# Shifted-window attention stage: scores in 32x64 tiles in two groups, transposes in two row tiles, group norm folded into projections, half of the maxima subtracted by GpSimd

## The chip, the cores and the metric

The kernel runs on one core of a Trainium2 chip. The metric is the time of one launch in microseconds (us). Engines are written as in the profile: PE (TensorE), PEld (its weight loads), DVE (VectorE), ACT (ScalarE), POOL (GpSimd), SP (the queue that issues the DMAs).

## The reference

The input is 16 images of 56x56 positions with 192 channels. Two blocks follow each other. The first, which the change does not touch, is a group norm, a layer norm, a scan over the 49 positions of each 7x7 window and an MLP. The second, cut to what matters:

```python
x = x + L1(gn(x))                       # gn: 32 groups of 6 channels, per image
# L1: windows of 7x7 shifted by 3, 12 heads of 16 dimensions
qkv  = xw @ qkv_w.T + qkv_b             # 1024 windows x 49 tokens x 576
attn = einsum('bhnd,bhmd->bhnm', q * 16**-0.5, k) + bias + mask
attn = softmax(attn, axis=-1)
out  = einsum('bhnm,bhmd->bhnd', attn, v) @ proj_w.T + proj_b
```

## The kernel before

The first block runs for some 2430 us. The second has 128 units of eight windows each (`UNITS`); a unit u has four steps p = 0 to 3 (`UP`), each with two windows of 49 tokens that lie in 64-row slots. Below, k = 4u + p numbers the steps. Every engine runs its own `slot(i, c, r)` once per unit, its instructions in the order in which they are written, and they meet by semaphores that count up; there is no scheduler. The engines work on different steps at a time. In step k:

- PE computes the scores of step k (line 1208: six matmuls, each of four heads of one window, with 64 rows and 64 columns of the array, 196 columns out), transposes the probabilities of step k-2 (line 1216), does a share of the next unit's projections (`project`, line 1159, `values`, line 1171), of the turning of its input (`turn`, line 1147) and of the last unit's output projection (`mix`, line 1190), and multiplies the probabilities of k-2 with the values (line 1251). A float32 matmul stands in the trace as two matmul records, a transpose or an fp32r matmul as one.
- DVE makes logits from scores of k (line 1082, `s_lg`), row maxima (line 1086, `s_mx`), row sums of the exponentials of k-1 (line 1090), their reciprocals (line 1092, `s_ri`), subtracts the maxima of k (line 1095, `s_sub`), and then does one or more tasks of the neighbour units: `finish` (line 1071), `lower` (line 1050), `queries_b` (line 1059), a copy of V (line 1109).
- ACT takes the exponential of k-1 (line 960), copies the transposed probabilities of k-2 to SBUF (line 969, `s_ptc`), empties projections (lines 941 and 947), and adds the value bias to the heads' output of k-2 (line 988, `s_o`).
- POOL multiplies the exponentials of k-1 by the reciprocals (line 885, `norm`, `s_nm`), and once per unit adds the output bias to the input (line 898); in steps 2 and 3 it scales and shifts the input of unit u+2 by the group norm's factors (lines 906 and 911).

The tables of the group norm are made once, in front of the units: DVE and POOL work out a factor and a shift per group, eight DMAs lay them out in DRAM (line 813), and each unit loads them back over all partitions (line 824).

## Time and profile before

| | |
|---|---|
| median of 3 runs | 4776.58 us (4773.7 to 4777.52) |
| the profiled execution's own time | 4771.56 us |
| its span, first to last instruction | 4769.8 us |
| granted clock of the core, mean | 0.990 |
| PE busy over the span | 4471.3 us (94%) |
| DVE busy | 4085.7 us (86%) |
| POOL busy | 2642.9 us (55%) |
| ACT busy | 2351.8 us (49%) |

Busy time of an engine is the time in which at least one of its instructions runs; a matmul's end is modelled, so a busy PE is not PE at its peak. A row of the timeline gives the start, the length and the count of instructions of one kind that follow each other on one engine, and in brackets how long the engine stood idle before them and who released it. The stretch of the units' steady course is 2510 to 4745 us of the span.

### The profile page before, as it was taken

To read this page: it belongs to the slowest core of one execution; us is meant where nothing else is said; L and a number is where in the kernel's file an instruction comes from. 1 tells how busy PE (TensorE), PEld (TensorE's weight loads), DVE (VectorE), ACT (ScalarE), POOL (GpSimd) and SP (SyncE) were. 2 spreads that over 40 slices of the span, in tenths; PEclk is the share of its full clock that TensorE was granted. 3 is DMA by queue.
4 is the path that set the end of the run, shared out by engine and by line. 5 is a ranking of instruction groups with operands and counts; after the bars stand their busy time and mean duration, and the time that the engine had idled before them with its cause. 6 is when DMAs were issued, how large, how long until landed. Compare 5 with 4: busy or idle time off the path is not lost. (4 is left out here: it accounts for less than half of the span.)

```text
span 4769.8 us, 122473 instructions
## 1 busy us (share of the span) xinstructions
PE 4471.3 (94%) x42440; PEld 3822.0 (80%) x42440; DVE 4085.7 (86%) x7841; ACT 2351.8 (49%) x4594; POOL 2642.9 (55%) x1714
## 2 busy tenths in 40 slices
PE   0599999999999999999969999999999999999998
PEld 0488888888888888888857888888888888888887
DVE  6798888888888888888838888888888888888887
ACT  0244444444444444444415555555555555555555
POOL 1245555455545554555536666666666666666665
PEclk9999999999999999999969999999999999999999
DMA  8011111111111111111112222222222222222222
GB/s 341 21 38 38 39 39 41 37 39 39 41 37 39 39 41 38 38 39 39 37 46 79 80 78 79 81 81 77 80 79 81 77 81 78 82 80 78 79 81 65
DMA packets 398996, 310.66 MB, mean 65 GB/s; under 512 B 140011, under 2 KB 397243, under 8 KB 397755
## 3 DMA queue, kind: packets, MB, share of 16 engines
q1 hardware_dynamic: 396212, 307.89, 21.9%
q10 hardware_dynamic: 2736, 2.14, 0.1%
q8 instruction: 29, 0.48, 0.0%
q14 instruction: 19, 0.16, 0.0%
HBM read 145.48 MB, written 87.33 MB: 49 GB/s over the span
## 5 line engine op out<-in xcount | busy, mean ns | idle before, releaser
L885 POOL TENSOR_TENSOR E<-E,ri 128x588 f32<-128x588 f32 x512 | 802.8, 1568 | 781.5 <-DVE ri L1092 781.5
L604 PE MATMUL ps_o<-w,g_hi 128*128 128x384 f32 x2352 | 709.7, 365 | 5.9 <-DVE g_lo L544 4.1
L416 ACT ACTIVATE gF<-ps_g,b1f 128x512 f32<-128x512 f32 x588 | 404.6, 688 | 392.8 <-PE ps_g L635 390.7
L604 PE MATMUL ps_o<-w,g_lo 128*128 128x192 f32 x2352 | 534.5, 254 | 0.0
L969 ACT ACTIVATE PT<-ps_t 98x588 f32<-98x588 f32 x512 | 338.9, 662 | 395.6 <-PE ps_t L1216 395.6
L1082 DVE SCALAR_TENSOR_TENSOR L<-ps_s,bias 128x588 f32<-128x588 f32 x512 | 394.6, 771 | 152.3 <-PE ps_s L1208 144.2
L1216 PE MATMUL ps_t<-ident,E 128*98 128x128 f32 x3072 | 441.8, 280 | 78.5 <-POOL E L885 78.4
L443 POOL TENSOR_TENSOR res<-xt,b2b 128x768 f32<-128x768 f32 x98 | 181.0, 1847 | 591.1 <-DVE x L492 591.1
L1216 PEld LDWEIGHTS ps_t<-ident,E 128*98 128x98 f32 x3072 | 313.8, 128 | 233.4 <-POOL E L885 198.1
L402 ACT ACTIVATE h_hi<-ps_h,hbias 128x512 fp32r<-128x512 f32 x196 | 123.1, 679 | 703.6 <-PE ps_h L619 703.6
L1208 PE MATMUL ps_s<-Kp,Q 64*64 64x196 f32 x6144 | 455.1, 342 | 2.7 <-DMA Kp<-K 2.7
L604 PEld LDWEIGHTS ps_o<-w,g_hi 128*128 128x128 f32 x2352 | 429.2, 189 | 26.6 <-issue 24.8
L604 PEld LDWEIGHTS ps_o<-w,g_lo 128*128 128x128 f32 x2352 | 443.4, 191 | 0.0
L988 ACT ACTIVATE oT<-ps_v,bqkv 128x98 f32<-128x98 f32 (+1 forms) x1024 | 289.1, 334 | 285.8 <-PE ps_v L1251 263.9
L1086 DVE TENSOR_REDUCE mx<-L 128x12 f32<-128x588 f32 x512 | 392.2, 766 | 17.5
L1090 DVE TENSOR_REDUCE sm<-E 128x12 f32<-128x588 f32 x512 | 386.5, 755 | 0.0
L1190 PE MATMUL ps_w<-wp,oT 128*98 128x192 f32 x2048 | 385.9, 332 | 0.7 <-ACT oT L988 0.7
L960 ACT ACTIVATE E<-L 128x588 f32<-128x588 f32 x512 | 351.9, 687 | 46.0 <-DVE L L1095 46.0
L1095 DVE TENSOR_TENSOR L<-L,mx 128x588 f32<-128x588 f32 x512 | 362.3, 708 | 0.0
L453 POOL TENSOR_TENSOR g_lo<-gF,g_hi 128x512 fp32r<-128x512 f32 x196 | 250.3, 1298 | 197.0 <-ACT g_hi L421 197.0
L421 ACT ACTIVATE g_hi<-gF 128x512 fp32r<-128x512 f32 x588 | 355.3, 621 | 0.0
L1251 PE MATMUL ps_v<-PT,Vx 98*32 98x49 f32 x12288 | 352.0, 232 | 3.1 <-issue 2.4
(203 smaller groups left out, 12238.8 us busy)
## 6 DMA issues: line engine op xcount, KB each, us to landing
xs<-in_x SPq DMA_DIRECT2D x8, 4704.0 KB, 22.3
xt<-in_x SPq DMA_DIRECT2D x98, 384.0 KB, 3.4
x_cells<-x SPq DMA_DIRECT2D x784, 48.0 KB
xb<-x_cells SPq DMA_DIRECT2D x128, 294.0 KB
Vx<-V SPq DMA_DIRECT2D x512, 73.5 KB
out<-yo SPq DMA_DIRECT2D x128, 294.0 KB
Kp<-K SPq DMA_DIRECT2D x512, 49.0 KB, 1.8
gnr<-gn_rows SPq DMA_DIRECT2D x128, 192.0 KB
```

Of the source, the lines that this page charges most:

```text
L416: act.activation(gF[f % 4][:, :], ps_g[:, f % 2, :], ACT.Gelu, bias=b1f[:, f:f + 1]).then_inc(s_gelu, 1)
L421: act.activation(g_hi[:, g, :], gF[g % 4][:, :], ACT.Copy).then_inc(s_gh, 1)
L604: last = pe.matmul(dst, g[:, f, P * k:P * (k + 1)], w, start=(f == 0 and i == 0), stop=(f == FT - 1 and i == 1))
L885: pool.tensor_tensor(e, e, ri[p][:, :].unsqueeze(2).to_broadcast([P, HEADS, T]), ALU.mult)\
L1082: dve.scalar_tensor_tensor(out=L[p][:, :, :].rearrange("p (a h) m -> p a (h m)", a=3), in0=s_block(slice(0, 3)), scalar=HD ** -0.5, in1=ta ...
L1086: dve.tensor_reduce(mx[p][:, :], L[p][:, :, :], AX.X, ALU.max).then_inc(s_mx, 1)
L1090: dve.tensor_reduce(sm[pp][:, :], E[pp][:, :, :], AX.X, ALU.add).then_inc(s_sm, 1)
L1095: dve.tensor_tensor(L[p][:, :, :], L[p][:, :, :], mx[p][:, :].unsqueeze(2).to_broadcast([P, HEADS, T]), ALU.subtract).then_inc(s_sub, 1)
L1190: last = pe.matmul(ps_w(OUT1 if half else OUT0)[0:T2, C * a:C * (a + 1)], oT[d][p][:, k, :], wp[:, k, :], start=(k == 0), stop=(k == 1))
L1208: last = pe.matmul(s_block(b)[SLOT * w:SLOT * (w + 1)], Q[c][rows, chunk, 2 * p + w, :], Kp[c][rows, chunk, :, 2 * p + w, :], start=True, ...
L1216: last = pe.transpose(ps_t[0:T2, j // JB, P * (j % JB):P * (j % JB + 1)], E[lp][:, 2 * j:2 * j + 2, :].rearrange("p h m -> p (h m)"), iden ...
L1251: last = pe.matmul(ps_v[row:row + 2 * HD, col:col + T], Vx[lc][0:T2, 2 * lp + w, j:2 * HD * JP:JP], PT[lp % 2][0:T2, j, T * w:T * (w + 1)] ...
```

## The change

- **Scores.** Six matmuls of four heads become twelve of two heads: 32 rows, 64 columns, 98 columns out (`scores`). They are issued in two groups: pairs 0, 3, 1, 4 (eight matmuls, signalled by `s_scx`) and pairs 2, 5 (four, `s_sc`). Q, K and the bias table have another order of heads for it, and K is spread over two copies, not four.
- **Transposes.** Six of 128 rows become twelve of 64 rows, 98 columns of weights and 64 columns moving, in two row tiles that write to two banks.
- **Order on PE.** In a step the first group of scores comes first, then `mix`, `project` or `values`, then the wait for the probabilities of k-2, then the second group of scores, then the transposes. The wait for the logits ahead of line 1251 goes; the wait for Q and K moves from the end of a unit to the start of the next.
- **Group norm.** The factor is applied where the turned input is emptied (ACT's scale, a scalar_tensor_tensor on DVE), the shift is projected once per image and added to the biases of Q, K and V. The two POOL instructions per unit, the tables in DRAM and their load go; a load of 7 numbers per partition and a 128x2 addition on POOL per unit come, and ahead of the units 18 small matmuls stand before the ones that gather the bias table.
- **Maxima.** DVE subtracts them from six heads; POOL from the other six, behind `norm` of k-1. ACT's exponential waits for both.

PE, around the end of a unit and the start of the next, before. `ps_s` holds scores, `ps_t` transposed probabilities, `ps_v` heads' outputs, `ps_w` projections; L1171 is `values`, L1190 is `mix`:

```order
L1208 MATMUL ps_s<-Kp,Q 64x196 x6
L1216 MATMUL ps_t<-ident,E 98x128 [waits probs_copied,probabilities]
L1216 MATMUL ps_t<-ident,E 98x128 x5
L1164 REGISTER_ALU
L1171 MATMUL ps_w<-wqkv_a_hi,x_hi 98x192 [waits queries_keys_masked]
...
L1251 MATMUL ps_v<-PT,Vx 32x49 [waits heads_ready,probs_copied,logits]
L1251 MATMUL ps_v<-PT,Vx 32x49 x11
...
L1190 MATMUL ps_w<-wp,oT 98x192 [waits queries_keys_masked,heads_ready]
L1190 MATMUL ps_w<-wp,oT 98x192 x3
L1208 MATMUL ps_s<-Kp,Q 64x196 x6
L1213 ISA
L53 REGISTER_ALU [waits probabilities]
```

The same place now (L1174 scores, L1214 `values`, L1271 transposes, L1298 values product, L1233 `mix`):

```order
L1174 MATMUL ps_s<-Kp,Q 64x98 x7
...
L1214 MATMUL ps_w<-wqkv_a_hi,x_hi 98x192 [waits queries_keys_masked]
...
L1265 REGISTER_ALU [waits probs_copied,probabilities]
L1174 MATMUL ps_s<-Kp,Q 64x98 [waits scores_first_rows_summed]
L1174 MATMUL ps_s<-Kp,Q 64x98 x3
L1271 MATMUL ps_t<-ident,E 98x64 x12
L1298 MATMUL ps_v<-PT,Vx 32x49 [waits heads_ready,probs_copied]
L1298 MATMUL ps_v<-PT,Vx 32x49 x11
...
L1233 MATMUL ps_w<-wp,oT 98x192 [waits queries_keys_masked]
```

The wait for the probabilities now stands ahead of scores, `values` has moved from between the transposes and the values product to ahead of that wait, and in step 3 nothing is left between the transposes and the values product.

POOL, one unit from its step 0, before (E is `norm`):

```order
L885 TENSOR_TENSOR E<-E,ri 128x588 [waits row_reciprocals]
L53 REGISTER_ALU [waits unit_loaded1]
L898 TENSOR_TENSOR rs<-xb,pbb 98x768 [waits unit_out_ready]
...
L885 TENSOR_TENSOR E<-E,ri 128x588 [waits row_reciprocals]
L53 REGISTER_ALU [waits unit_loaded1]
L906 TENSOR_TENSOR xn_u<-xb,gnr 98x768 [waits unit_transposed]
L883 REGISTER_ALU
L885 TENSOR_TENSOR E<-E,ri 128x588 [waits row_reciprocals]
L910 REGISTER_ALU
L911 TENSOR_TENSOR xn_u<-xn_u,gnr 98x768 [waits unit_scaled]
```

And now:

```order
L883 TENSOR_TENSOR E<-E,ri 128x588 [waits row_reciprocals]
L887 ISA
L889 TENSOR_TENSOR L<-L,mx 128x294 [waits row_maxima]
L54 REGISTER_ALU [waits unit_loaded1]
L904 TENSOR_TENSOR rs<-xb,pbb 98x768 [waits unit_out_ready]
L883 TENSOR_TENSOR E<-E,ri 128x588 [waits row_reciprocals]
L887 REGISTER_ALU
L889 TENSOR_TENSOR L<-L,mx 128x294 [waits row_maxima]
...
L912 TENSOR_TENSOR vb<-par,bqkv 128x2 [waits heads_ready,queries_b_masked]
```

Behind every `norm` there is now a subtraction of the maxima of the following step, and the group norm's two instructions are gone.

The core of the diff:

```diff
 # GpSimd
+                def less_max(u, p):
+                    pool.wait_ge(s_mx, UP * u + p + 1)
+                    l = L[p][:, HS:HEADS, :]
+                    pool.tensor_tensor(l, l, mx[p][:, HS:HEADS].unsqueeze(2).to_broadcast([P, HEADS - HS, T]),
+                                       ALU.subtract).then_inc(s_sbp, 1)
...
                         if is_unit(pu):
                             norm(pu, pp)
+                        if is_unit(u):
+                            less_max(u, p)
...
-                                pool.tensor_tensor(xn[0:T2, :, :], xb[c][0:T2, :, :],
-                                                   gnr[c][0:T2, 0:C].unsqueeze(1).to_broadcast([T2, UP, C]), ALU.mult)\
...
+                            pool.tensor_tensor(vb[d][:, :], par[d][:, 5:7], bqkv[:, 3:5], ALU.add).then_inc(s_vb, 1)
 # ScalarE
                             act.wait_ge(s_sub, k + 1)
+                            act.wait_ge(s_sbp, k + 1)
                             upto(act, s_pt, k - 3)
                             act.activation(E[pp][:, :, :], L[pp][:, :, :], ACT.Exp).then_inc(s_ex, 1)
 # VectorE, lower()
-                    dve.tensor_tensor(dst, ps_w(TURN + h)[rows, 0:UW], x_hi[rows, h, :],
-                                      ALU.subtract).then_inc(s_xl, 1)
+                    dve.scalar_tensor_tensor(out=dst, in0=ps_w(TURN + h)[rows, 0:UW], scalar=par[1 - c][rows, h:h + 1],
+                                             in1=x_hi[rows, h, :], op0=ALU.mult, op1=ALU.subtract).then_inc(s_xl, 1)
 # VectorE, slot()
-                            dve.tensor_tensor(L[p][:, :, :], L[p][:, :, :],
-                                              mx[p][:, :].unsqueeze(2).to_broadcast([P, HEADS, T]),
+                            l = L[p][:, 0:HS, :]
+                            dve.tensor_tensor(l, l, mx[p][:, 0:HS].unsqueeze(2).to_broadcast([P, HS, T]),
                                               ALU.subtract).then_inc(s_sub, 1)
 # TensorE
+                def scores(c, p, places):
+                    for j in places:
+                        rows, chunk = pair_rows(PAIR_AT[j])
+                        for w in range(2):
+                            last = pe.matmul(s_pair(j)[SLOT * w:SLOT * (w + 1)], Q[c][rows, chunk, 2 * p + w, :],
+                                             Kp[c][rows, chunk, :, 2 * p + w, :], start=True, stop=True)
+                    return last
...
                         if is_unit(u):
-                            for w, b in ((0, 0), (0, 2), (1, 0), (1, 2), (0, 1), (1, 1)):
-                                row, chunk = key_block(b)
-                                rows = slice(row, row + HB * HD)
-                                last = pe.matmul(s_block(b)[SLOT * w:SLOT * (w + 1)], Q[c][rows, chunk, 2 * p + w, :],
-                                                 Kp[c][rows, chunk, :, 2 * p + w, :], start=True, stop=True)
-                            last.then_inc(s_sc, 1)
-                        if is_unit(lu):
-                            k = UP * u + p - 2
-                            pe.wait_ge(s_nm, k + 1)
-                            upto(pe, s_ptc, k)
-                            for j in range(JP):
-                                last = pe.transpose(ps_t[0:T2, j // JB, P * (j % JB):P * (j % JB + 1)],
-                                                    E[lp][:, 2 * j:2 * j + 2, :].rearrange("p h m -> p (h m)"),
-                                                    ident[:, :])
-                            last.then_inc(s_pt, 1)
+                            upto(pe, s_lg, UP * u + p)
+                            scores(c, p, (0, 3, 1, 4)).then_inc(s_scx, 1)
                         if is_unit(u - 1) and p == 0:
                             mix(i, c, 0)
                         if nxt:
...
                                 project(i, c, 2)
                             if p == 3:
                                 values(i, c, 1)
+                        if is_unit(lu):
+                            pe.wait_ge(s_nm, UP * u + p - 1)
+                            upto(pe, s_ptc, UP * u + p - 2)
+                        if is_unit(u) and between:
+                            pe.wait_ge(s_scx, UP * u + p + 1)
+                            scores(c, p, (2, 5)).then_inc(s_sc, 1)
+                        if is_unit(lu):
+                            for j in range(JP):
+                                for w in range(2):
+                                    rows = slice(SLOT * w, SLOT * (w + 1))
+                                    last = pe.transpose(ps_t[0:T2, w, SLOT * j:SLOT * (j + 1)],
+                                                        E[lp][rows, 2 * j:2 * j + 2, :].rearrange("p h m -> p (h m)"),
+                                                        ident[rows, rows])
+                            last.then_inc(s_pt, 1)
...
-                            if is_unit(u):
-                                pe.wait_ge(s_lg, UP * u + p + 1)
```

`between` is true in all but the first and the last units.

## Rows read from the trace of the kernel before

**Rows 1.** Windows: length, PE, PEld, DVE, ACT, POOL busy, granted clock, DMA share, GB/s.
```profile
2510.00:4745.00 2235.00, 2158.35 (x28776) 1829.72 (x28777) 1958.76 (x3298) 1314.69 (x2788) 1472.02 (x886) 1.00 0.28 79
4750.00:4755.00 5.00, 2.82 (x47) 1.90 (x44) 4.48 (x8) 2.45 (x5) 1.57 (x1) 1.00 0.01 3
4755.00:4760.00 5.00, 4.88 (x42) 4.47 (x43) 2.35 (x6) 1.52 (x5) 1.57 (x1) 0.66 0.01 5
```

**Rows 2.** Groups, 2510 to 4745 us: shapes, count, busy us, mean ns, idle before.
```profile
L885 POOL TENSOR_TENSOR E<-E,ri 128x588 f32<-128x588 f32 x508 | 796.9, 1569 | 773.9 <-DVE ri L1092 773.9
L1216 PE MATMUL ps_t<-ident,E 128*98 128x128 f32 x3042 | 437.0, 280 | 76.7 <-POOL E L885 76.6
L1095 DVE TENSOR_TENSOR L<-L,mx 128x588 f32<-128x588 f32 x508 | 359.4, 708 | 0.0
L898 POOL TENSOR_TENSOR rs<-xb,pbb 98x768 f32<-98x768 f32 x126 | 231.2, 1835 | 0.0
```

**Rows 3.** Timeline of one unit from its step 0: start us, length us, what.
```profile
3507.46 0.89 PE L1208 MATMUL ps_s<-Kp,Q 64*64 64x196 f32 x12
3508.39 0.77 DVE L1082 SCALAR_TENSOR_TENSOR L<-ps_s,bias 128x588 f32<-128x588 f32 x1 [0.27 <-PE ps_s L1208]
3510.70 0.69 PE L1251 MATMUL ps_v<-PT,Vx 98*32 98x49 f32 x24
3510.97 1.57 POOL L885 TENSOR_TENSOR E<-E,ri 128x588 f32<-128x588 f32 x1 [1.27 <-DVE ri L1092]
3511.32 0.53 PE L1147 MATMUL ps_w<-ident,xn_u 98*64 98x98 f32 x4
3512.48 0.56 DVE L1050 TENSOR_TENSOR x_hi<-ps_w,x_hi 64x392 fp32r<-64x392 f32 x1
3512.60 0.86 PE L1216 MATMUL ps_t<-ident,E 128*98 128x128 f32 x6
3513.48 0.34 PE L1159 MATMUL ps_w<-x_lo,wqkv_a_hi 128*128 128x392 f32 x1
3514.91 0.34 PE L1159 MATMUL ps_w<-x_hi,wqkv_b_lo 128*128 128x392 f32 x1
3516.39 0.68 ACT L960 ACTIVATE E<-L 128x588 f32<-128x588 f32 x1
3516.97 0.57 ACT L947 ACTIVATE K<-ps_w,bqkv 128x392 f32<-128x392 f32 x1
3525.06 0.89 PE L1208 MATMUL ps_s<-Kp,Q 64*64 64x196 f32 x12
```

**Rows 4.** Timeline ahead of that unit, from its predecessor's step 3.
```profile
3505.99 1.54 PE L1190 MATMUL ps_w<-wp,oT 128*98 128x192 f32 x8
3506.20 0.71 DVE L1095 TENSOR_TENSOR L<-L,mx 128x588 f32<-128x588 f32 x1
3506.36 1.57 POOL L885 TENSOR_TENSOR E<-E,ri 128x588 f32<-128x588 f32 x1 [1.13 <-DVE ri L1092]
3507.02 0.69 ACT L960 ACTIVATE E<-L 128x588 f32<-128x588 f32 x1 [0.35 <-DVE L L1095]
3507.89 1.81 POOL L911 TENSOR_TENSOR xn_u<-xn_u,gnr 98x768 f32<-98x768 f32 x1
3509.25 0.66 ACT L969 ACTIVATE PT<-ps_t 98x588 f32<-98x588 f32 x1 [1.54 <-PE ps_t L1216]
```

**Rows 5.** Narrow windows of the timeline, scores of step 1.
```profile
3511.78 0.40 PE L1208 MATMUL ps_s<-Kp,Q 64*64 64x196 f32 x4
...
3512.00 0.67 PE L1208 MATMUL ps_s<-Kp,Q 64*64 64x196 f32 x8
```

**Rows 6.** Groups of the first block: DVE with and without a pointer scalar, POOL.
```profile
L482 DVE SCALAR_TENSOR_TENSOR h_lo<-ps_h,hbias,h_hi 128x512 fp32r<-128x512 f32 x98 | 73.6, 751 | 15.8 <-ACT h_hi L402 15.1
L480 DVE TENSOR_TENSOR y_lo<-ps_g,y_hi 128x512 fp32r<-128x512 f32 x98 | 67.8, 692 | 4.2 <-ACT y_hi L392 1.2
L176 POOL TENSOR_TENSOR wA_b_lo<-raw_A,wA_b_hi 128x192 fp32r<-128x192 f32 x1 | 0.6, 597 | 0.0
```

More of the change, by code:

```diff
@@ L940, in evacuated @@
                         upto(act, s_sc, UP * (v - 1))
-                        last = act.activation(Q[d][:, 0, :, 0:T], full, ACT.Identity, bias=bqkv[:, 0:1])
+                        last = act.activation(Q[d][:, 0, :, 0:T], full, ACT.Identity, bias=par[d][:, 2:3])
                     else:
@@ L947, in evacuated @@
                         last = act.activation(K[0:rows, k, :, :], full[0:rows], ACT.Identity,
[L948 removed]
+                                              bias=par[d][0:rows, 2 + m:3 + m])
                     last.then_inc(s_qkm, 1)
@@ L1023, in _ @@
+                last.then_inc(s_par, 1)
                 link(dve.memset(base[:, :, :], 0.0))
@@ L1228, in slot @@
                                 values(i, c, 1)
+                        if is_unit(lu):
[12 more added lines that the diff above has]
+                            last.then_inc(s_pt, 1)
                         if nxt and p == 0:
                             turn(i, c, 0)
+                        if is_unit(u) and not between:
+                            pe.wait_ge(s_scx, UP * u + p + 1)
+                            scores(c, p, (2, 5)).then_inc(s_sc, 1)
                         if nxt and p == 1:
@@ L1333 @@
     arrays["b1"] = by_column(inputs["L0_conv_b1"], rows=P)[:, :, 0]
-    def by_dimension(block):
-        return CB * block + np.array([HD * e + d for d in range(HD) for e in range(CB // HD)])
-    first, second = np.r_[by_dimension(0), by_dimension(2)], by_dimension(1)
+    by_dimension = np.array([2 * HD * g + HD * e + d for g in range(JP) for d in range(HD) for e in range(2)])
+    first, second = by_dimension[0:P], by_dimension[P:C]
     by_parity = np.array([HD * (2 * j + e) + d for e in range(2) for d in range(HD) for j in range(JP)])
@@ L1345 @@
     arrays["proj_b"] = plain("L1_conv_proj_b")
-    arrays["rpb"] = plain("L1_conv_rpb_table")
+    arrays["rpb"] = np.ascontiguousarray(plain("L1_conv_rpb_table")[:, [2 * g + e for g in PAIR_AT for e in range(2)]])
     arrays.update(shape_constants())
```

179 lines of the change are left out of this document (102 added, 77 removed).

## The prediction

> **What bounds the kernel now.** I read the windows first. The change lies in the 128 units, and 2510 to 4745 us of the span is their steady course: PE is busy 2158 of 2235 us, DVE 1959, and the clock is granted in full [rows 1]. The group of line 898 has one instruction per unit, so 126 units lie there [rows 2]; from one unit's scores to the next it is 3525.06 - 3507.46 = 17.60 us [rows 3]. PE is nearly full, but not alone: it idles 76.7 us ahead of the transposes, all of it for POOL's `norm` [rows 2], that is 0.6 us per unit. So PE work counts, and so does every chain that ends in a wait of PE. Then I read the timeline of one unit for the two relations that the new order touches. First, scores of step k stand on PE ahead of the wait for `norm` of k-2; they and DVE's logits run while `norm` is still busy: `norm` 3506.36 to 3507.93, scores from 3507.46, logits at 3508.39 [rows 3, 4]. Second, the exponential of k-1 starts 0.11 us after DVE's subtraction ends (3506.20 + 0.71, then 3507.02), which is before `norm` of the step before is done (3507.93) [rows 4]. ACT then waits 1.54 us for the transposes: the exponential costs the transposes' copy nothing.
>
> **PE's own work.** In the scores, four matmuls run at a time: four records start at 3511.78 and the next at 3512.00; those eight end at 3512.67, a record lasts 0.32, so the last starts at 3512.35 [rows 5]. After the first round, which has 0.05 us of weight load ahead, rounds of 196 columns come 0.17 us apart. A round of 98 columns is 0.08, the same per column. The first group now takes 0.05 + 4 x 0.08 = 0.39 us of the array, the second 0.05 + 2 x 0.08 = 0.22, together 0.61 against 0.05 + 4 x 0.17 = 0.73. That holds if tiles of 32 rows run four at a time as those of 64 do; no row shows it, so the other end is two at a time: 0.72 and 0.39. The transposes: six of 128 columns take 0.70 now; twelve of 64 columns in two row tiles are bound by weights of 98 columns, about 0.09 us each, as six pairs 0.55, one by one 1.05. I take 0.55. It will not matter, see below.
>
> Between kinds of tile there is a gap. The last scores' record of 3512.35 has streamed by 3512.52, and the transposes start at 3512.60 [rows 3, 5]: 0.08 to 0.1, plus 0.05 for a weight load that nothing covers. Counted by the listing there are 14 such changes per unit before, and 25 now, since the scores are cut in two and the transposes have a tile of their own: 11 x 0.14 = 1.5 us. The Trainium skill (TensorEngine Tiling (Array Packing), "Key Properties") says that changing the tiling mode drains the engine; the trace agrees, with that gap. PE's work thus goes from 17.0 to 17.0 - 4 x 0.12 - 4 x 0.15 + 1.5 = 17.4 us per unit: nothing is gained there.
>
> **The moved wait.** Now the second group of scores of step k stands behind the wait for `norm` of k-2. The logits of k need it, and the order on DVE is logits, maxima, sums of k-1, reciprocals of k-1, which `norm` of k-1 needs. That closes a ring over one step: from logits to the start of `norm` 3510.97 - 3508.39 = 2.58; `norm` 1.57; its end at 3512.54 to PE 0.06 [rows 3]; second group to logits 0.44 (load 0.05, first round 0.08, then a record of 98 columns: its stream 0.08 and the 0.16 by which a record outlasts its stream, 0.05 to DVE). B = 4.64 us for a step that may take 17.60 / 4 = 4.40 now. Queued behind PE's wait: scores, transposes, values product; DVE waits for the first.
>
> **The shared maxima.** POOL's half of 588 columns stands behind `norm` of k-1, and ACT's exponential waits for it. Its length: 192 columns take 597 ns [rows 6], 588 take 1569 [rows 2]; on the line between, 294 columns take 0.84; with the broadcast's slope, 0.88. The low end is half of 1569, 0.78. I take 0.88. The Trainium skill (GPSIMD Engine Reference, "3.1 Elementwise — side-by-side cycle accounting") gives 4497 ns for 2048 columns, which would make an estimate of 0.65 us; the sum by it would be 0.23 us per unit, 29 us in all, lower. Its "4.1 Engine selection" keeps elementwise work on VectorE, GpSimd being about twice as slow: the trace agrees, 1569 against 708 ns for the same shape [rows 2]. DVE saves 4 x 0.29 us per unit. But the exponential of k-1 now starts `norm` 1.53 + 0.88 + 0.11 after `norm`'s start instead of 0.66 (3507.02 - 3506.36) [rows 4], and in ACT's order the copy of the transposed probabilities of k-2 stands behind it. The values product waits for that copy. In step 3 nothing stands between transposes and product on PE any more, and what followed them before (`values`) is done already; so PE idles there, and the rest of the step and `mix` of the next queue behind.
>
> **The sum.** I follow the longest chain over one unit, from logits of step 0 to logits of the next step 0.
> A, step 0 to 1: logits to the end of the last `lower` 3513.04 - 3508.39 = 4.65 [rows 3]; the half subtraction -0.29; `lower` is now a scalar_tensor_tensor with a pointer, 751 against 692 ns [rows 6], twice: +0.12; to PE 0.06; `project`, whose matmuls are (3514.91 - 3513.48) / 8 = 0.18 apart [rows 3], five and a load 0.94; gap 0.09; second group to logits 0.44. It used to be hidden: scores and transposes stood ahead of `project`; now only the first group does. A = 6.01.
> B, step 1 to 2: the ring, 4.64.
> C, steps 2 and 3: logits to `norm` 2.58; to the next POOL instruction 1.53 (3507.89 - 3506.36); 0.88; 0.11; exponential 0.69; the copy 0.66, less 0.10 by which an ACT instruction starts ahead of its predecessor's end (3516.39 + 0.68 against 3516.97) [rows 3]; 0.05; values product 0.62 (3510.70 to 3511.32); `mix` 1.47 (3505.99 to 3507.46) [rows 3, 4]; first group 0.48 with gap; `mix` of step 0, 1.47; second group to logits 0.44. C = 10.88.
> Unit: 21.53 us, +3.93. Times 126: +495 us. PE is idle for some 4 us of each unit, in pieces of about 1 us.
> Ahead of the units, 18 small matmuls at half clock, which also wait for the weights, now stand before the bias gathering: I allow +6 us (0 to 10, no row resolves it). The fewer K and group norm DMAs have slack and are put at nothing. Removing POOL's two instructions per unit is worth nothing: it idled 773.9 us for DVE [rows 2], and it is not their place that the chain passes. The whole is 4771.56 + 501 = 5273 for the profiled execution; the median of the runs lies 5 us higher, so **5278 us**.
> Low end of the sum: POOL's half 0.78, no cost for the pointer, half subtraction 0.35, the groups 0.09 shorter each (four of them), a load hidden ahead of each `mix`: 20.8, 5190 us. High end: below.
>
> **Rivals.**
> 1. Tiles of 32 rows run only two at a time: first group +0.33, second +0.17 in A, B and C: 22.4 us per unit, 5385 us. For it: no row shows 32-row tiles. Against: scores of 64 rows and products of 32 columns do overlap. Chance 0.12, in the range.
> 2. Only the ring binds, the copy is in time: 4 x 4.64 = 18.56 us, +121 + 6: 4904 us. It needs ACT to reach the copy before the exponential; its written order is against it. 0.10.
> 3. Not slower: PE's work sets the pace, as it does for most of the unit now. With 17.4 us, 4776.6 - 25 + 6 = 4757 us. It decides if PE arrives at the moved wait later than `norm` ends in all four steps, so that neither the ring nor the copy shows. For it: PE is 97% busy. Against: PE already waits 0.6 us per unit for `norm`. 0.07.
> 4. The clock: at the span's end PE at 2.82 of 5 us busy still had the full clock, and had 0.66 right after [rows 1]. PE would be 81% busy. If it fell to the lower level for good, the 5.2 us of PE in the chain double: 26.7 us, 5930 us. 0.03.
>
> **Numbers.** The forecast has 0.68 (5130 to 5420). With rival 1 the range holds 0.80. Slower 0.93, faster 0.05, within 0.2% (what a measurement of this kernel tells from no change, some 10 us) 0.02.
>
> **What would show it.** Right: scores' groups 0.39 and 0.22 us long; a unit of 21 to 22 us; PE idle ahead of the values product, released by the copy, over 1 us in step 3, and ahead of the second group, released by `norm`; ACT's exponential released by POOL's half in nearly all of the steps; POOL's half 0.8 to 0.9 us; DVE idle ahead of the logits; the first block unchanged. Wrong: a unit under 19 us, an exponential released by DVE, a PE without idle time, or a lower clock in the steady stretch.

## The result, and the profile after

The changed kernel takes 5712.34 us (median of 4 runs, 5710.07 to 5721.75), the kernel before 4777.05 beside it: ratio 1.196 (95% interval 1.194 to 1.198). The forecast was 5278, range 5130 to 5420. The direction was right, the size was not: 434 us are missing. The profiled execution took 5721.75 us, with a span of 5719.9 and a mean granted clock of 0.865.

The first view is again the windows (bounds; length; busy time and instructions of PE, PEld, DVE, ACT, POOL; granted clock; DMA share; GB/s). The first two rows are the first block, before and now; the third is a stretch of the units, to be held against [rows 1]:

```profile
0.00:2430.00 2430.00, 2257.07 (x13180) 1944.18 (x13180) 2087.28 (x4491) 1021.15 (x1775) 1140.30 (x803) 1.00 0.17 53
0.00:2430.00 2430.00, 2256.92 (x13180) 1943.77 (x13180) 2096.61 (x4491) 1021.86 (x1775) 1140.18 (x803) 1.00 0.17 53
3000.00:4000.00 1000.00, 874.35 (x11881) 688.61 (x11874) 567.70 (x1034) 409.58 (x874) 378.98 (x398) 0.77 0.17 48
```

The first block is as it was. In the units the granted clock is 0.77 on average: stretches at 2.4 GHz (1.00 in these rows) and at 1.2 GHz (0.50) take turns. PE is busy 87%, but busy at a slower clock. A unit lasts 25.0 us (17.6 before), and its length goes with the clock of its stretch. Four windows of 25 us of the same kernel:

```profile
3500.00:3525.00 25.00, 21.63 (x325) 17.16 (x317) 15.29 (x29) 10.78 (x24) 10.46 (x11) 0.86 0.18 52
3720.00:3745.00 25.00, 21.66 (x310) 16.66 (x309) 14.28 (x26) 10.22 (x23) 10.54 (x11) 0.84 0.17 48
3845.00:3870.00 25.00, 20.85 (x325) 16.50 (x325) 15.37 (x29) 10.92 (x23) 12.07 (x13) 0.93 0.17 48
4040.00:4065.00 25.00, 23.42 (x230) 18.68 (x231) 10.56 (x20) 8.26 (x17) 8.32 (x10) 0.52 0.17 45
```

The last one does some two thirds of the work of the others (20 DVE instructions against 26 to 29) with PE busier than ever. Measured from one addition of line 904 to the next, the 21 units with a clock of 0.9 to 0.99 last 22.17 us on average, the 18 with 0.60 last 29.5 us. Two shorter windows show a change from the one level to the other:

```profile
3867.40:3870.00 2.60, 1.94 (x26) 1.50 (x26) 0.91 (x2) 0.70 (x1) 2.33 (x2) 1.00 0.00 0
3870.80:3887.80 17.00, 16.24 (x181) 13.01 (x179) 8.26 (x16) 6.38 (x16) 5.84 (x7) 0.50 0.15 43
```

Ahead of this fall PE had stood idle for 1.65 us, until 3868.06 (its row follows below). The lower level then stays for 17 us, though PE is busy for 16.24 of them.

In the third window the chain itself can be read nearly without the clock. Its timeline (start, length, idle before and releaser) has DVE's logits first, then what PE waits for, with `norm` (L883) and the second groups of scores (L1174, x8):

```profile
3848.26 0.77 DVE L1098 SCALAR_TENSOR_TENSOR L<-ps_s,bias 128x588 f32<-128x588 f32 x1 [2.52 <-PE ps_s L1174]
3853.02 0.77 DVE L1098 SCALAR_TENSOR_TENSOR L<-ps_s,bias 128x588 f32<-128x588 f32 x1 [1.28 <-PE ps_s L1174]
3857.46 0.77 DVE L1098 SCALAR_TENSOR_TENSOR L<-ps_s,bias 128x588 f32<-128x588 f32 x1 [1.16 <-PE ps_s L1174]
3863.46 0.77 DVE L1098 SCALAR_TENSOR_TENSOR L<-ps_s,bias 128x588 f32<-128x588 f32 x1 [1.77 <-PE ps_s L1174]
3869.62 0.77 DVE L1098 SCALAR_TENSOR_TENSOR L<-ps_s,bias 128x588 f32<-128x588 f32 x1 [1.69 <-PE ps_s L1174]
```
```profile
3850.84 1.26 POOL L883 TENSOR_TENSOR E<-E,ri 128x588 f32<-128x588 f32 x1 [3.31 <-DVE ri L1108]
...
3852.55 0.40 PE L1174 MATMUL ps_s<-Kp,Q 32*64 32x98 f32 x8
...
3855.60 1.26 POOL L883 TENSOR_TENSOR E<-E,ri 128x588 f32<-128x588 f32 x1 [2.86 <-DVE ri L1108]
...
3857.00 0.40 PE L1174 MATMUL ps_s<-Kp,Q 32*64 32x98 f32 x8
3857.33 0.54 PE L1271 MATMUL ps_t<-ident,E 64*98 64x64 f32 x12
3858.89 0.73 PE L1298 MATMUL ps_v<-PT,Vx 98*32 98x49 f32 x24 [1.02 <-ACT PT L970]
...
3861.02 0.57 PE L1174 MATMUL ps_s<-Kp,Q 32*64 32x98 f32 x16
...
3868.06 0.45 PE L1202 MATMUL ps_w<-x_hi,wqkv_a_hi 128*128 128x392 f32 x1 [1.65 <-DVE x_hi L1066]
```

Logits to logits: 4.76 (B), 4.44 + 6.00 = 10.44 (C), 6.16 (A); 21.36 us in all, where 4.64, 10.88 and 6.01 = 21.53 were forecast. PE waits 1.02 us for the copy in step 3, and 1.65 us for `lower` in step 1, which A has in it. So the chain as a whole was right (B for another reason than forecast, see the late wait below), and what is missing is the clock. Why it fell is what the experiments had to find: the waits, or the small tiles?

POOL's groups of 3500 to 4500 us, against [rows 2], show two sizes that were off (busy, mean ns of one, idle before and its releaser):

```profile
L883 POOL TENSOR_TENSOR E<-E,ri 128x588 f32<-128x588 f32 x160 | 201.9, 1262 | 622.2 <-DVE ri L1108 622.2
L889 POOL TENSOR_TENSOR L<-L,mx 128x294 f32<-128x294 f32 x159 | 107.1, 673 | 0.0
```

### The profile page after: what moved, and what is told of

It reads as the page before. It is cut to its first block, busy times and chain, and to the rows that moved or that the text cites. A ratio compares the mean times of both kernels' runs of the same rounds, so it can differ in the third digit from the quotient of the medians.

```text
span 5719.9 us, 140981 instructions
## 1 busy us (share of the span) xinstructions
PE 5092.5 (89%) x51720; PEld 4181.5 (73%) x51720; DVE 3941.9 (69%) x7850; ACT 2344.3 (41%) x4594; POOL 2374.8 (42%) x2098
## 4 chain that ended last, share of the span: by engine, by line
issue 37%; POOL 13%; PE 4%; ACT 2%; DVE 1%; POOLq 0%; SPq 0%; DMA 0%; ACTq 0%; DVEq 0%
POOL L L889 5%; POOL E L883 4%; POOL rs L904 4%; PE ps_v L1298 1%; ACT PT L970 1%; PE ps_w L1202 1%; ACT oT L990 1%; PE ps_w L1233 1%; PE ps_s L1174 0%; POOL vb L912 0%; POOLq L887 0%; PE ps_s L1161 0%; PE ps_s L1162 0%; PE ps_t L1271 0%; SPq L808 0%
## 5 line engine op out<-in xcount | busy, mean ns | idle before, releaser
L883 POOL TENSOR_TENSOR E<-E,ri 128x588 f32<-128x588 f32 x512 | 646.1, 1262 | 1972.9 <-DVE ri L1108 1972.9
L1174 PE MATMUL ps_s<-Kp,Q 32*64 32x98 f32 x12288 | 599.4, 304 | 20.5 <-POOL E L883 17.8
L1174 PEld LDWEIGHTS ps_s<-Kp,Q 32*64 32x64 f32 x12288 | 362.3, 158 | 258.8 <-issue 217.9
L1298 PE MATMUL ps_v<-PT,Vx 98*32 98x49 f32 x12288 | 393.6, 249 | 175.4 <-ACT PT L970 123.9
L1298 PEld LDWEIGHTS ps_v<-PT,Vx 98*32 98x32 f32 x12288 | 324.5, 152 | 279.9 <-ACT PT L970 153.8
L1233 PE MATMUL ps_w<-wp,oT 128*98 128x192 f32 x2048 | 525.1, 413 | 1.6 <-ACT oT L990 0.9
L990 ACT ACTIVATE oT<-ps_v,vb 128x98 f32<-128x98 f32 (+1 forms) x1024 | 289.0, 334 | 415.3 <-PE ps_v L1298 415.3
L603 PEld LDWEIGHTS ps_o<-w,g_hi 128*128 128x128 f32 x2352 | 429.6, 189 | 26.7 <-issue 24.8
L1233 PEld LDWEIGHTS ps_w<-wp,oT 128*98 128x98 f32 x2048 | 402.6, 210 | 56.4 <-issue 21.6
L1202 PE MATMUL ps_w<-x_hi,wqkv_a_hi 128*128 128x392 f32 x384 | 221.9, 578 | 212.6 <-DVE x_hi L1066 212.6
```

What stands on the lines that cost most here:

```text
L603: last = pe.matmul(dst, g[:, f, P * k:P * (k + 1)], w, start=(f == 0 and i == 0), stop=(f == FT - 1 and i == 1))
L883: pool.tensor_tensor(e, e, ri[p][:, :].unsqueeze(2).to_broadcast([P, HEADS, T]), ALU.mult)\
L1174: last = pe.matmul(s_pair(j)[SLOT * w:SLOT * (w + 1)], Q[c][rows, chunk, 2 * p + w, :], Kp[c][rows, chunk, :, 2 * p + w, :], start=True, s ...
L1233: last = pe.matmul(ps_w(OUT1 if half else OUT0)[0:T2, C * a:C * (a + 1)], oT[d][p][:, k, :], wp[:, k, :], start=(k == 0), stop=(k == 1))
L1298: last = pe.matmul(ps_v[row:row + 2 * HD, col:col + T], Vx[lc][0:T2, 2 * lp + w, g:2 * HD * JP:JP], PT[lp % 2][0:T2, j, T * w:T * (w + 1)] ...
```

## The experiments

Each table row is one kernel: its median, the granted clock and PE's busy share from 3000 to 4000 us, and the mean unit. In the old order with old scores the program has no wait between the two groups. The parts are those of the change: order of PE, scores' tiles (S), transposes' tiles (T), maxima shared or on DVE alone.

| kernel | order | S | T | maxima | us | clock | PE busy | unit |
|---|---|---|---|---|---|---|---|---|
| before | old | old | old | DVE | 4777 | 1.00 | 97% | 17.62 |
| changed | new | new | new | shared | 5712 | 0.77 | 87% | 25.02 |
| late wait | new, B ahead of the wait | new | new | shared | 5706 | 0.78 | 87% | 24.84 |
| maxima back | new | new | new | DVE | 5751 | 0.79 | 86% | 25.19 |
| old tiles | new | old | old | shared | 5437 | 0.94 | 87% | 22.66 |
| new transposes | new | old | new | shared | 5519 | 0.88 | 86% | 23.38 |
| new scores | new | new | old | shared | 5476 | 0.89 | 88% | 23.06 |
| full-tile filler | new | new | new | shared | 5497 | 0.99 | 93% | 23.22 |
| small-tile filler | new | new | new | shared | 6023 | 0.81 | 96% | 27.36 |
| half the full filler | new | new | new | shared | 5247 | 1.00 | 92% | 21.23 |
| old order | old | new | new | DVE | 4854 | 1.00 | 94% | 18.17 |
| fold alone | old | old | old | DVE | 4811 | 1.00 | 96% | 17.85 |
| fold, new scores | old | new | old | DVE | 4893 | 1.00 | 95% | 18.49 |
| fold, maxima | old | old | old | shared | 4773 | 1.00 | 98% | 17.54 |
| transposes moved | half new | old | old | shared | 5009 | 1.00 | 90% | 19.39 |
| scores moved | half new | old | old | shared | 6111 | 0.87 | 76% | 27.99 |
| fold, maxima, transposes | old | old | new | shared | 4759 | 1.00 | 96% | 17.41 |
| no fold, maxima, transposes | old | old | new | shared | 4739 | 1.00 | 96% | 17.32 |

Two more things differ between these kernels. All but "before", "changed" and "maxima back" have an empty instruction on PE (`pe.nop`) ahead of the transposes and, but for the last kernel, ahead of each group of scores; what it costs is measured under "Fold, maxima, tiles by themselves". And all but "before" and the last have the changed kernel's waits of PE: none for the logits ahead of the values product, the one for Q and K at the start of a unit.

### Waits or tiles

The second group of scores (B in the table) ahead of the moved wait, and the maxima back on DVE:

```diff
-                            pe.wait_ge(s_nm, UP * u + p - 1)
-                            scores(c, p, (2, 5)).then_inc(s_sc, 1)
+                            scores(c, p, (2, 5)).then_inc(s_sc, 1)
+                            pe.wait_ge(s_nm, UP * u + p - 1)
```

> The changed kernel, with one edit: where the second group of scores stands behind the wait for the probabilities, it is put ahead of that wait. Measured of the changed kernel: 5712 us, a unit of 25.0 us at a mean granted clock of 0.77, about 21.4 us where the clock is nearly full. Theory of the chain: the ring over one step opens, so the step 1 to 2 loses its 4.64 us and follows PE's work; B falls by 0.3 to 0.5 us, C by up to 0.4, and the unit at full clock to 20.5 to 21.0. Theory I (the clock falls because PE idles in the waits; idle time is taken from the unit's length): the clock rises only with the little idle time that goes, to 0.77 to 0.82; 5550 to 5690 us. Theory F (the clock falls because of the small tiles, whatever the idle time): the clock stays at 0.75 to 0.79; 5620 to 5700 us. This run says what the ring is worth, not which of the two holds.

Measured 5706.24 us (ratio 1.195, 1.192 to 1.199): nothing is gained, so the ring over the wait isn't what binds with this order. In the timeline above, the second group of 3852.55 starts 0.45 us after `norm` is done (3850.84 + 1.26 = 3852.10), behind `project`; only that of 3857.00 comes close behind it (3855.60 + 1.26 = 3856.86). The forecast overrated the ring. This kernel has the empty instructions, and its clock is 0.78 against 0.77: they don't bring the clock back.

> The changed kernel, with the subtraction of all twelve maxima back on DVE, none on POOL; order and tiles stay. Theory of the chain: the exponential no longer waits for norm and POOL's half, so the copy of the transposed probabilities is not held up; C loses up to 1.5 us, DVE's longer subtraction gives 0.29 back in A, B and C: unit at full clock 20.0 to 21.2 (against about 21.4). Rival: the order alone holds PE, and the shared maxima cost nothing: 21.4 or more, since DVE is longer. Theory I: the clock rises with what idle time goes, 5450 to 5650 us. Theory F: clock 0.75 to 0.79, 5550 to 5700 us.

Measured 5750.54 us (1.204, 1.201 to 1.208): 38 us slower, against the theory of the chain. What PE waits for from 3500 to 4500 us (total, times, longest), in the changed kernel and in this one:

```profile
PE ps_w L1202 <- DVE x_hi L1066: 66.5, 40, 1.7
PE ps_v L1298 <- ACT PT L970: 37.2, 40, 1.0
```
```profile
PE ps_w L1199 <- DVE x_hi L1063: 78.6, 40, 2.0
PE ps_v L1295 <- ACT PT L967: 30.4, 40, 0.8
```

The wait for the copy is 0.17 us per unit shorter, as the theory had it, but the wait for `lower`, behind DVE's longer subtraction, is 0.30 us longer.

The tiles of before in the new order, and the new tiles in the order of before (with all maxima on DVE). Of the first edit, the transposes:

```diff
-                                for w in range(2):
-                                    rows = slice(SLOT * w, SLOT * (w + 1))
-                                    last = pe.transpose(ps_t[0:T2, w, SLOT * j:SLOT * (j + 1)], E[lp][rows, ...
+                                last = pe.transpose(ps_t[0:T2, j // JB, P * (j % JB):P * (j % JB + 1)], E[lp][:, ...
```

> The changed kernel's order, waits, shared maxima and folded group norm, with the tiles of the kernel before: scores in tiles of 64 rows and 64 columns (first group the four matmuls of two blocks, here eight matmuls in all ahead and four behind), transposes of 128 rows. Theory F (small tiles make the clock fall): the clock is granted in full, the unit is 21 to 22 us long as the chain has it, 5200 to 5330 us. Theory I (idle time of PE makes it fall): the waits and the idle time are the same, the clock is 0.75 to 0.85 as in the changed kernel, 5550 to 5750 us.

> The order of PE as in the kernel before (both groups of scores, then the wait for the probabilities, then the transposes, then mix or project), all maxima on DVE; the new tiles and the folded group norm stay. Theory I (idle time): PE has no more idle time than before, so the clock is granted in full and the unit is 17.2 to 17.9 us: 4740 to 4830 us. Theory F (tiles): PE is as busy, but the clock falls to 0.75 to 0.9; the 17 us of PE's work stretch to 19 to 22 us: 4950 to 5350 us.

Measured 5437.18 (1.139, 1.135 to 1.142) and 4854.44 us (1.017, 1.014 to 1.020). Neither theory holds alone. The windows of the two:

```profile
3000.00:4000.00 1000.00, 868.65 (x10007) 649.08 (x10009) 630.66 (x1149) 457.04 (x970) 420.25 (x441) 0.94 0.19 53
```
```profile
3000.00:4000.00 1000.00, 937.36 (x16456) 784.83 (x16455) 853.62 (x1433) 582.79 (x1211) 452.07 (x331) 1.00 0.24 67
```

With the same busy share of 87%, the clock is 0.94 with the old tiles and 0.77 with the new ones; with PE busy 94%, the new ones cost no clock at all. The loss comes with waits and small tiles together. Split by kind of tile:

> The changed kernel's order, waits and shared maxima, with the scores in the old tiles of 64 rows and 64 columns, and the transposes in the new ones of 64 rows. With both kinds of tile old the time was 5437 us at a clock of 0.95 in the units, with both new 5712 at 0.78. Theory S (the scores' tiles of 32 rows make up the difference): near the first, 5420 to 5500 us, clock 0.92 to 0.95. Theory T (the transposes' tiles do): near the second, 5600 to 5700 us. If each takes part by its time on PE, about 5550 us, clock 0.86.

> The other half: the changed kernel's order, waits and shared maxima, with the new scores of 32 rows, and the transposes as before with all 128 rows. Theory S: 5620 to 5712 us, clock 0.76 to 0.82. Theory T: 5430 to 5500 us, clock 0.92 to 0.95. If both take part, about 5550 us. The two halves together also say whether the effects add: the losses of clock, 0.17 in all, should then sum to it.

Measured 5519.19 (1.156, 1.153 to 1.159) and 5476.43 us (1.147, 1.144 to 1.150): clocks of 0.88 and 0.89. Both kinds take part, 0.06 and 0.05 of the 0.17; the two together lose more than the sum.

### Filling the waits

```diff
+                        for _ in range(7):   # in project, ahead of the wait for the lower parts
+                            pe.matmul(ps_w(QK)[:, 0:C], ident[:, :], wp[:, 0, :], start=True, stop=True)
                         pe.wait_ge(s_xl, 2 * v + 2)
...
+                                for _ in range(5):   # step 3, ahead of the wait for the copy
+                                    pe.matmul(ps_v[:, 0:C], ident[:, :], wp[:, 0, :], start=True, stop=True)
                             pe.wait_ge(s_ptc, k + 1)
```

> The changed kernel, with PE's two long waits of each unit filled: seven matmuls of 128 rows by 128 columns of weights and 192 columns ahead of the wait for the lower parts (PE idles 1.65 us there), five ahead of the wait for the copied probabilities of step 3 (1.0 us); 0.18 us each by the rows of mix, 2.2 us in all. Their results are overwritten; the output is the same. The chain isn't longer by more than 0.2 us per unit at full clock. Theory I (idle time of PE takes the clock away): the clock is 0.95 to 1.00 and the unit 21.2 to 22.0 us; 5200 to 5350 us. Theory F (the small tiles take it away, whatever else runs): the clock stays at 0.75 to 0.85, the fillers take twice their time in half of the stretches; 5650 to 5850 us. Theory A (what counts is how much of the array has been at work, summed over all work): full tiles fill it, so as in theory I.

Small tiles: `[0:64, 0:C], ident[0:32, 0:64], wp[0:32, 0, :]`, as many.

> As the filler with full tiles, but each of the twelve filling matmuls uses a tile of 32 rows by 64 columns of weights, one at a time, with the same 192 columns and so the same 0.18 us each. PE's idle time is filled alike, the array is used one sixteenth... one eighth as much. Theory I (idle time): the clock comes back as with full tiles, 0.95 to 1.00, 5200 to 5350 us. Theory A (how much of the array is at work): the clock stays where it was, 0.75 to 0.82, 5650 to 5800 us. Theory F: the same as A, or lower.

Measured 5497.13 us (1.151, 1.148 to 1.155) with full tiles and 6023.21 (1.262, 1.258 to 1.265) with small ones. The windows, full first:

```profile
3000.00:4000.00 1000.00, 932.42 (x13946) 775.36 (x13947) 617.43 (x1125) 442.22 (x952) 412.66 (x433) 0.99 0.19 52
```
```profile
3000.00:4000.00 1000.00, 956.54 (x11793) 738.67 (x11789) 521.54 (x950) 373.86 (x804) 348.17 (x366) 0.81 0.16 44
```

This is the pair that decides. Both kernels run the same instructions with the same columns, some 323 records per unit, and at the full clock a filler's record lasts 326 ns with full tiles and 319 at the least with small ones. PE has less idle time with the small fillers (956.54 us busy) than with the full ones (932.42), and yet the clock is 0.81 against 0.99. So the busy share does not set the clock; with the rest alike, it goes with how much of the array the fillers use. Theories I and F fall, A is the one that is left. The fillers were twice as long as forecast: each matmul is two records of 0.16 us, so they outlasted the waits, and both times lie outside their ranges. Hence half of the full ones, four and two:

> The changed kernel with half of the full-tile fillers: four ahead of the wait for the lower parts, two ahead of the wait for the copy of step 3. In the first filler kernel each matmul took two passes of 0.17 us and not 0.18 in all, so the fillers outlasted the waits by 1.6 us per unit, at a clock of 0.99: 5497 us. Now 1.3 and 0.65 us, both shorter than the waits at full clock (1.65, 1.0). Theory A: the clock is 0.92 to 1.00 in the units and the unit 21.3 to 22.3 us, so that the time is 5240 to 5380 us, near the chain as it was forecast without a loss of clock. If the fillers must outlast the waits to hold the clock: 0.80 to 0.90, 5400 to 5600 us.

Measured 5246.63 us (1.099, 1.097 to 1.101):

```profile
3000.00:4000.00 1000.00, 924.35 (x14652) 749.08 (x14654) 672.23 (x1225) 481.26 (x1036) 450.38 (x473) 1.00 0.20 57
```

Twelve records of work that nobody uses make the changed kernel 466 us faster. With the clock in full the unit is 21.23 us: 21.53 was forecast for it, and 5278 for the whole.

### Which move costs

At full clock the new order still costs some 4 us per unit. From the kernel with fold and shared maxima (old tiles, 17.54 us), one move at a time:

```diff
 (transposes moved)                               (scores moved)
  scores(c, p, (0, 3, 1, 4))                       scores(c, p, (0, 3, 1, 4))
+ scores(c, p, (2, 5))                             wait for norm; transposes
  mix, project or values                           mix, project or values
  wait for norm                                  + scores(c, p, (2, 5))
- scores(c, p, (2, 5)); transposes                 values product
```

> One half of the new order alone, with the folded group norm, the shared maxima and the tiles of before: both groups of scores stand ahead of mix, project or values, the wait for the probabilities and the transposes behind them. The old order with these parts has a unit of 17.54 us, the new one 21.78 where the clock is full. In the forecast's chain, this half makes the copy of the transposed probabilities late: C keeps its copy and values product (0.56 + 0.05 + 0.62 us), but the second group and its logits no longer stand in A, B and C. If the moved second group is the main cost: unit 17.6 to 19.0 us, 4780 to 4960 us. If the late transposes are: 20 to 21.5 us, 5080 to 5300 us. I expect 18.5 us.

> The other half alone, same parts otherwise: first group of scores, then the wait for the probabilities and the transposes as before, then mix, project or values, and behind them the second group of scores. In the forecast's chain A keeps its 6.0 us (logits, maxima, lower, project, second group), the ring of B closes over PE all the same, since first group, transposes and project stand between, C loses the late copy. If the moved second group is the main cost: unit 20 to 21.5 us at full clock, 5080 to 5300 us, more if the clock falls. If the late transposes are: 17.6 to 19.0 us. I expect 20.5 us. If the two halves add, this unit and the other half's, less 17.54 each, sum to 4.24 us.

Measured 5008.85 us (1.049, 1.047 to 1.051) and 6110.88 (1.279, 1.277 to 1.282). The halves do not add: +1.85 us per unit for the transposes, +10.4 for the scores (at a clock of 0.87), and +4.24 for both at full clock (the old-tiles kernel's units above 0.95 of clock last 21.78). The first lies between its two ranges, the second above both, and not by the clock alone: a step of 6.25 us at a clock of 0.98 stands below. With the scores alone moved, PE waits for `norm` in each of the 143 steps of 1000 us:

```profile
PE ps_t L1259 <- POOL E L883: 246.5, 143, 2.0
```
```profile
3510.15 0.83 PE L1259 MATMUL ps_t<-ident,E 128*98 128x128 f32 x6 [1.84 <-POOL E L883]
...
3511.81 0.55 PE L1175 MATMUL ps_s<-Kp,Q 64*64 64x196 f32 x4
...
3516.40 1.49 PE L1259 MATMUL ps_t<-ident,E 128*98 128x128 f32 x6 [1.86 <-POOL E L883]
```

That is the ring the forecast had drawn as B, with transposes and `project` inside it: 3516.40 - 3510.15 = 6.25 us per step. The 20.5 us expected for it left them out. The changed kernel has `project` ahead of the wait for `norm` and the transposes behind the second group, so neither is in its ring.

### Fold, maxima, tiles by themselves

> Of the change only the folded group norm stays: no multiplication and subtraction on POOL per unit, the scale and the bias in the copies, lower as a scalar_tensor_tensor; order, tiles and maxima as in the kernel before. The prediction put the removed POOL work at nothing, since POOL idled for DVE. But norm took 1262 ns in the changed kernel where it took 1569 before, and PE waited 33.6 us per 1000 us for it: 0.6 us per unit. If norm is shorter for good: 0.3 to 0.6 us less per unit, 4700 to 4750 us. If the slower lower (0.12 us per unit on DVE) is all that is left: 4775 to 4800 us.

> The folded group norm and the maxima shared with POOL, in the order and with the tiles of before. It takes DVE's subtraction from 0.70 to 0.40 us and sets the exponential behind norm and POOL's half (0.67 us). In this order the copy of the transposed probabilities has slack of more than 1 us ahead of the values product. If the shared maxima are hidden: within 10 us of the same kernel without them. If DVE's 0.29 us per step bound it: up to 60 us faster than that. If norm, now queued ahead of the half, starts later for it: 20 to 100 us slower. I expect 20 us slower.

> The folded group norm, PE's order, the maxima and the transposes as before; the scores in tiles of 32 rows, whose second group has to wait for the end of the first. With the transposes' tiles new as well this was 4854 us, unit 18.17 us, clock 1.00, with PE idle 0.18 us between the two groups in every step (0.72 us per unit). If that wait is what the new tiles cost in this order: 4830 to 4870 us, and the clock in full, since PE is 93% busy. If the transposes' tiles cost as much: 4790 to 4820 us. Theory A (use of the array): no loss of clock here, as with all tiles new.

Measured 4810.89 (1.008, 1.006 to 1.009), 4772.55 (0.999, 0.998 to 1.000) and 4893.46 us (1.025, 1.023 to 1.027). The kernel with the fold alone is 34 us slower, outside both of its ranges: 29 us in the units (0.23 x 126), so some 5 ahead of them; its `norm` takes 1568 ns as before. The shared maxima give 38 us back, where a loss of 20 was expected. The scores' small tiles cost 83, again outside both ranges. The program has the second group, which uses other rows for the same banks, wait for the first one's end (`s_scx`); no run is without that wait. PE's waits show its price (total, times, longest):

```profile
PE ps_s L1172 <- PE ps_s L1172: 38.7, 216, 0.2
```

216 steps in 1000 us, 0.18 each: 0.72 us per unit, against 0.64 measured. The transposes in two row tiles then gain 39 us (4893 to 4854).

Most of the 34 us is not the fold. `norm` and the transposes that wait for it, before and in the kernel with the fold alone:

```profile
3515.66 1.57 POOL L885 TENSOR_TENSOR E<-E,ri 128x588 f32<-128x588 f32 x1 [1.33 <-DVE ri L1092]
3517.28 0.86 PE L1216 MATMUL ps_t<-ident,E 128*98 128x128 f32 x6 [0.59 <-POOL E L885]
```
```profile
3520.89 1.57 POOL L883 TENSOR_TENSOR E<-E,ri 128x588 f32<-128x588 f32 x1 [1.55 <-DVE ri L1105]
3522.60 0.83 PE L1258 MATMUL ps_t<-ident,E 128*98 128x128 f32 x6 [0.70 <-POOL E L883]
```

The transposes start 0.05 us after `norm` ends before, and 0.14 us after with the empty instruction ahead of them; over the steady stretch these are the shortest distances of the two kernels. In the steps without a wait the distance from scores to transposes is 0.82 us in both, so the empty instruction costs nothing there. In two steps of each unit of the fold kernel the transposes start at that distance, which makes an estimate of 2 x 0.09 x 126 = 23 us of the 34.

What the shared maxima change is in the groups of POOL and DVE from 3500 to 4500 us, without sharing and with it:

```profile
L883 POOL TENSOR_TENSOR E<-E,ri 128x588 f32<-128x588 f32 x224 | 351.3, 1568 | 539.5 <-DVE ri L1105 539.5
L1109 DVE TENSOR_TENSOR L<-L,mx 128x588 f32<-128x588 f32 x224 | 158.3, 707 | 0.0
```
```profile
L883 POOL TENSOR_TENSOR E<-E,ri 128x588 f32<-128x588 f32 x228 | 287.8, 1262 | 455.4 <-DVE ri L1108 455.4
L1112 DVE TENSOR_TENSOR L<-L,mx 128x294 f32<-128x294 f32 x228 | 91.5, 401 | 0.0
```

`norm` and DVE's subtraction run side by side, the subtraction first, as in the changed kernel here:

```profile
3850.68 0.40 DVE L1112 TENSOR_TENSOR L<-L,mx 128x294 f32<-128x294 f32 x1
3850.84 1.26 POOL L883 TENSOR_TENSOR E<-E,ri 128x588 f32<-128x588 f32 x1 [3.31 <-DVE ri L1108]
```

DVE's gets shorter by 306 ns, and `norm`, whose own work is the same, by 306 ns too. So POOL stands still while DVE subtracts. The Trainium skill (SBUF — State Buffer, "Who interferes with whom") says that a DVE instruction with two SBUF inputs contends with a GpSimd one that reads SBUF, and that the order of issue decides which of two is blocked; the trace agrees, to the nanosecond. How much of the 38 us is DVE's own 0.31 us per step and how much `norm`'s was not taken apart. The transposes also follow `norm` at 0.14 us in one step less per unit, so that some 11 us of them (0.09 x 126) may be the empty instruction's.

The parts that paid, in the old order:

```diff
 (before, and)
+                        if is_unit(u):
+                            less_max(u, p)
...
-                            for j in range(JP):
-                                last = pe.transpose(ps_t[0:T2, j // JB, ...
+                            for j in range(JP):
+                                for w in range(2):
+                                    last = pe.transpose(ps_t[0:T2, w, ...
```

> A version of the parts that paid in the old order: folded group norm, shared maxima, transposes in two row tiles; the order of PE and the scores' tiles as in the kernel before. The steps measured: fold +34.5, shared maxima -38.3, transposes' tiles -39.0 (4854.4 against 4893.5) beside 4776.35. If they add: 4733.5 us, 0.9% faster than before. If PE's wait for norm takes back what the transposes save: 4750 to 4772 us. Theory A (use of the array) has the clock in full, since PE is over 95% busy.

> The kernel before with the shared maxima and the transposes in two row tiles alone, without the fold. If the steps add: 4776.35 - 38.3 - 39.0 = 4699 us. If POOL, which keeps its two instructions of 1.83 us per unit, is late for its half of the maxima in steps 3 and 0, where the exponential waits behind 1.83 us more: 4710 to 4800 us. This tells what the fold is worth once POOL has its half: between this kernel and the last one.

Measured 4758.82 us with the fold (0.996, 0.995 to 0.998) and 4738.65 without it (0.992, 0.990 to 0.994), the fastest of all. The steps do not add in full: with the fold 4733 was the sum, without it 4699. The fold costs 20 us here, some 11 of them in the units (0.09 x 126), though it takes two POOL instructions of 1.8 us out of each unit. Both kernels have the empty instruction ahead of the transposes and wait for `norm` in one step per unit, so it is not in this difference.

## Why the prediction was wrong, point by point

- **The bound** ("PE is nearly full, but not alone"): right in the main. The moved scores and transposes showed up in the time, and so did 0.3 us on DVE and POOL; the late wait did not (5706 against 5712).
- **A, 6.01 us**: measured 6.16, with a granted clock of 1.00 over that stretch. Right, with its reason: PE waits for `lower` (1.65 us), then `project` and the second group.
- **B, 4.64 us**: its ring was mis-sized. `norm` is 1.26 and not 1.57, which makes it 4.33; measured is 4.76, and removing the ring changed nothing (late wait, 5706). What fills this step is PE's own work, `project` with its neighbours, without a gap, its start at a lower clock (0.61 from 3846.9 to 3850.3): that 4.64 came so near is luck. The ring binds when PE has more work inside it, as in the kernel with the scores alone moved.
- **C, 10.88 us**: with `norm` shorter by 0.31 and POOL's half at 0.67 instead of 0.88, it is 10.36; measured 10.44. Right, with its sign: the copy is late in step 3, and PE idles there for 1.02 us.
- **Tiles**: the groups of scores last 0.57 and 0.40 us, which is the 0.39 and 0.22 forecast and some 0.16 by which a record outlasts its stream; so tiles of 32 rows run four at a time, and rival 1 falls. The matmul behind the transposes starts 0.47 us after the first of them (3863.32 to 3863.79), where 0.55 was forecast. The price of the program's wait between the two groups was overlooked; in the new order other work hides it.
- **POOL's half, 0.88 us**: 0.67, below the range of 0.78 to 0.88. The line through [rows 6] and [rows 2] used a `norm` that stood still while DVE subtracted. The estimate by the Trainium skill, 0.65, was nearer.
- **POOL's removed work, nothing**: right about POOL. The fold itself costs 20 us in the old order, where both kernels have the empty instruction ahead of the transposes (4759 against 4739); `lower` with a pointer (0.12 us per unit, 15 us) and the prologue (+6) were counted, 21 in all. Of the 34 us of the fold alone, some 23 are the empty instruction.
- **The step that failed: "PE is idle for some 4 us of each unit, in pieces of about 1 us"**, and the sum's times of PE then taken at full clock. The clock in the units was 0.77, and the unit 25.02 us where 21.53 was forecast. The idle time was forecast; that it and the smaller tiles together would cost the clock stood only in rival 4, with a chance of 0.03. Its argument was the end of the span, where PE is at 2.82 of 5 us busy at a full clock [rows 1]. That was a few microseconds with the old tiles, and the very next row has 0.66; it said nothing of 3.2 ms with the new ones. The clock accounts for all of the 434 us: with the clock held by fillers the kernel takes 5247 us, 31 below the forecast.
- **Rival 4's own size** was off as well. It doubled 5.2 us of PE in the chain to get 26.7 us; units at a clock of 0.60 take 29.5. At that clock PE's 17.4 us of work alone make 29.0, and the waits close: that is the 23.42 of 25 us busy in the window at 4040. And the clock did not fall for good, but in stretches; why it comes back is not shown.

What stays open: whether rows, columns or the two together make a tile count for little, and whether the values in it matter; the fillers differ in rows and columns at once, and their weights, an identity, are mostly zeros in both. Nor does any run give the amount: the small fillers have 0.81 where the changed kernel without them has 0.77, so they are not nothing.

## What to carry to other kernels

Where a change gives PE more waits and smaller tiles at once, forecast the clock as a cost of its own: price the chain at both levels, and look at the array's use, since the busy share alone hides it. If such waits can't go, matmuls of full tiles in them can be worth their nuisance; the fillers shorter than the waits gained 466 us, those that outlasted them 215. When an operation of POOL starts beside one of DVE with two SBUF inputs, as `norm` does here, its length may contain the other's: shorten DVE's and POOL's shrinks with it. And a change of five parts should be timed part by part: here two paid (38 and 39 us), two cost, and the order lost an estimated 900 (5712 against 4854 - 38 in the old order), some 430 of it with the clock in full (5247). The probes should differ from their base in the part alone: an empty instruction made an estimated 23 us here, two thirds of what the fold seemed to cost.

## What the runs showed of the hardware

- The busy share alone does not set the granted clock: PE busy 96% with small fillers had 0.81, PE busy 90% with old tiles 1.00 (transposes moved), 76% with old tiles 0.87 (scores moved).
- The lower clock can last while PE is busy: 0.50 over 17 us with PE busy 16.24 of them.
- Useless full-tile work of 12 records of 0.16 us per unit brought the clock from 0.77 to 1.00 and the time from 5712 to 5247 us. The Trainium skill (TensorE: Matmul & The Clock Gate, "HAM oscillation — how this bites in real kernels") tells of a clock lost in waits for DMA longer than any here; the longest idle time in this chain is 1.7 us, and it oscillates all the same.
- POOL's `norm` of 588 columns took 1568 or 1262 ns, with a neighbour on DVE that took 707 or 401.
- An empty instruction on PE behind a wait that PE has to sit out puts the next matmul 0.09 us later (0.14 against 0.05 after `norm`'s end); where PE does not wait, it cost nothing.
